# The layer norm's last step moved from VectorE to ScalarE in a transformer layer kernel

## The reference

```python
def _layernorm(x, axis=-1, eps=1e-05):
    m = jnp.mean(x, axis=axis, keepdims=True)
    v = jnp.var(x, axis=axis, keepdims=True)
    return (x - m) / jnp.sqrt(v + eps)
...
        q = _low_rank_proj(hidden_states, q_a, q_b)
        k = _low_rank_proj(hidden_states, k_a, k_b)
        v = hidden_states @ v_w.T + v_b
...
        att = jnp.where(causal[None, None], att, jnp.finfo(att.dtype).min)
        att = jax.nn.softmax(att, axis=-1)
        y = jnp.einsum('bhts,bhsd->bhtd', att, v)
...
    xn = _layernorm(x, axis=-1)
    x = x + _L0_attn_ref(xn, ...) + _L0_ffn_ref(xn, ...)
```

## Time and profile before

| | us |
|---|---|
| median of 3 runs (1224.98, 1230.92, 1231.64) | 1230.92 |
| the profiled execution, device time | 1225.27 |
| its span from first to last instruction | 1223.5 |
| PE busy | 1156.1 (94%) |
| DVE busy | 1012.4 (83%) |
| ACT busy | 683.7 (56%) |
| GpSimd busy | 699.0 (57%) |

### The profile page before, as it was taken

The page is one execution under the profiler, slowest core; times in us unless marked ns, Lnnn a source line. Parts: engine busy times, 40 slices in busy tenths (PEclk is TensorE's granted clock), DMA queues, the critical chain, the costliest instruction groups (busy, mean ns, idle before and its releaser), DMA issues. The chain is left out here.

```text
span 1223.5 us, 26313 instructions
## 1 busy us (share of the span) xinstructions
PE 1156.1 (94%) x8558; PEld 808.0 (66%) x8558; DVE 1012.4 (83%) x3396; ACT 683.7 (56%) x1334; POOL 699.0 (57%) x1021
## 2 busy tenths in 40 slices
PE   7799999999999999999999998889999999999994
PEld 6455565565555655555555554459889999999994
DVE  4798998989889999999999978779966777676762
ACT  4367667667667676767676665634333433343330
POOL 1235445445445344355355367755888888888874
PEclk9799999999999999999999999989999999999997
DMA  7534244244254343443442453225655665566753
GB/s 164 149 114 114 77 142 132 68 139 133 73 139 116 95 122 106 122 122 95 131 124 81 133 145 114 64 76 128 129 119 112 129 137 115 113 132 132 104 76 46
DMA packets 140380, 139.43 MB, mean 114 GB/s; under 512 B 24908, under 2 KB 132052, under 8 KB 140244
## 3 DMA queue, kind: packets, MB, share of 16 engines
q1 hardware_dynamic: 109540, 102.07, 29.3%
q0 software_dynamic: 24576, 33.57, 16.4%
q10 hardware_dynamic: 6128, 2.11, 0.8%
HBM read 53.22 MB, written 33.55 MB: 71 GB/s over the span
## 5 line engine op out<-in xcount | busy, mean ns | idle before, releaser
L850 DVE CUSTOM_DVE_ANT_0 junk<-bank,rowmask 128x256 bf16<-128x256 f32 (+3 forms) x1024 | 445.7, 481 | 33.4 <-PE bank L1016 30.1
L700 ACT ACTIVATE probs<-bank 128x512 f32<-128x512 f32 x640 | 365.4, 595 | 126.1 <-PE bank L1039 121.0
L585 POOL TENSOR_SCALAR_AFFINE_SELECT probs<-probs 128x256 f32<-128x256 f32 (+1 forms) x640 | 227.7, 370 | 237.4 <-ACT probs L700 232.9
L1016 PE MATMUL bank<-kstk,qstk 96*128 96x256 bf16 (+3 forms) x1024 | 247.7, 304 | 12.6 <-DMA kstk<-qk_part 6.9
L1039 PE MATMUL bank<-qstk,kstk 98*128 98x256 bf16 (+3 forms) x1024 | 249.1, 306 | 2.6 <-ACT probs L700 1.6
L1203 POOL DMA_INDIRECT out_rows<-mixed,rows x128 | 210.9, 1648 | 61.2 <-issue 36.6
L1061 PE MATMUL bank<-probs,vaug 128*32 128x512 f32 (+3 forms) x2048 | 180.5, 448 | 7.6 <-POOL probs L585 7.6
L1227 ACT ACTIVATE hid<-bank 128x512 f32<-128x512 f32 x128 | 76.6, 598 | 173.6 <-PE bank L1320 172.7
L1039 PEld LDWEIGHTS bank<-qstk,kstk 98*128 98x128 bf16 x1024 | 75.6, 98 | 137.3 <-ACT probs L700 92.7
L1338 PE MATMUL bank<-w_hi,hid_hi 128*128 128x256 f32 x512 | 147.3, 288 | 0.0
L1338 PE MATMUL bank<-w_hi,hid_lo 128*128 128x256 f32 x512 | 144.9, 283 | 0.0
(11 more groups left out here) (157 smaller groups left out, 2167.1 us busy)
## 6 DMA issues: line engine op xcount, KB each, us to landing
qstk<-qk_part SPq DMA_DIRECT2D x192, 128.0 KB, 2.4
kstk<-qk_part SPq DMA_DIRECT2D x186, 128.0 KB, 2.7
qstk<-in_L_ffn_w SPq DMA_DIRECT2D x32, 512.0 KB, 4.2
xln<-in_L_attn_hidden_states SPq DMA_DIRECT2D x16, 512.0 KB, 5.0
xn_rows<-xn SPq DMA_DIRECT2D x16, 512.0 KB, 2.9
xres<-in_L_attn_hidden_states SPq DMA_DIRECT2D x16, 512.0 KB, 4.0
out_rows<-xres SPq DMA_DIRECT2D x16, 512.0 KB, 3.4
out_rows<-mixed,rows POOLq DMA_INDIRECT x128, 3.9
```

The source lines that it names most:

```text
L585: nc.gpsimd.affine_select(out=block, in_=block, compare_op=ALU.is_ge, fill=0.0, base=0, pattern=[[0, len(cols)], [1, P]], channel_multipli ...
L700: nc.scalar.activation(probs[n % 2][:, 512 * k:512 * k + 512], SCORET[k % 2][:], ACT.Exp, scale=SCALE).then_inc(exp_done, 1)
L850: last = nc.vector.tensor_tensor_reduce(out=junk[k % 2][:, col:col + width], in0=SCORE[score_bank(UN * n + k)][:, col:col + width], in1=ro ...
L1016: last = nc.tensor.matmul(SCORE[score_bank(UN * n + k)][:, col:col + width], qstk[b % 2][0:KS, GH * g + h, P * i:P * i + P], kstk[b % 2][0 ...
```

## The change

DVE no longer writes `xn`. A new step `lnshift` on DVE forms shift = -mean * rstd in one small instruction of 128x4. `lnapply` is now ACT's: four activations with the function Identity, `xn = rstd * xln + shift`, where `rstd` and `shift` are one number per row. `lnshift` stands in slot 2 of g = 1, `lnapply` stays in slot 4. Who waits for `xn` (SP's store, PE's transposes) still waits for `xn_done`.

```diff
-    [(4, "lnapply", 2, 0), (6, "v", 1, 3), (6, "o", -1, 1), (7, "o", -1, 2), (8, "o", -1, 3)],
+    [(2, "lnshift", 2, 0), (4, "lnapply", 2, 0), (6, "v", 1, 3), (6, "o", -1, 1), (7, "o", -1, 2), (8, "o", -1, 3)],
...
-    ... + foldt(1) + [("lnapply", 0, 0), ("xload", 1, 0), ("warm", 8, 0)]
+    ... + foldt(1) + [("lnshift", 0, 0), ("lnapply", 0, 0), ("xload", 1, 0), ("warm", 8, 0)]
...
-    out += [("wo", 0, 0), ("wo", 1, 0), ("v", 0, 2), ("v", 0, 3), ("lnapply", 1, 0)]
+    out += [("wo", 0, 0), ("wo", 1, 0), ("v", 0, 2), ("v", 0, 3), ("lnshift", 1, 0), ("lnapply", 1, 0)]
...
@@ ScalarE @@
+                        elif kind == "lnapply":
+                            act.wait_ge(shift_done, n + 1)
+                            if n >= 1:
+                                act.wait_ge(xn_stored, 16 * n)
+                                prev = ("xt", n - 1, 1)
+                                act.wait_ge(shared_ready[bank_of(prev)], filled(prev, at))
+                            for tt in range(TT):
+                                last = nc.scalar.activation(xn[:, tt, :], xln[:, tt, :], ACT.Identity, bias=shift[:, tt:tt + 1],
+                                                            scale=rstd[:, tt:tt + 1])
+                            last.then_inc(xn_done, 1)
...
@@ VectorE @@
-                        elif kind == "lnapply":
-                            dve.wait_ge(rstd_done, at(n + 1, 2))
+                        elif kind == "lnshift":
+                            dve.wait_ge(rstd_done, n + 1)
                             if n >= 1:
-                                dve.wait_ge(xn_stored, at(16 * n, 32))
-                                prev = ("xt", n - 1, 1)
-                                dve.wait_ge(shared_ready[bank_of(prev)], filled(prev, at))
-                            for tt in range(TT):
-                                last = nc.vector.tensor_scalar(xn[:, tt, :], xln[:, tt, :], meanvar[:, tt, 0:1],
-                                                               rstd[:, tt:tt + 1], ALU.subtract, ALU.mult)
-                            last.then_inc(xn_done, 1)
+                                dve.wait_ge(xn_done, n)
+                            nc.vector.scalar_tensor_tensor(out=shift[:], in0=meanvar[:, :, 0], scalar=-1.0, in1=rstd[:],
+                                                           op0=ALU.mult, op1=ALU.mult).then_inc(shift_done, 1)
```

More of the change, by code:

```diff
@@ L130, in prologue_steps @@
     out = [("warm", 16, 0), ("xload", 0, 0)] + foldt(0) + [("lnstat", 0, 0), ("lnstat", 0, 1)]
-    out += [("foldm", 0, 0), ("fold", 0, 0), ("warm", 8, 0)] + foldt(1) + [("lnapply", 0, 0), ("xload", 1, 0), ("warm", 8, 0)]
+    out += [("foldm", 0, 0), ("fold", 0, 0), ("warm", 8, 0)] + foldt(1) + [("lnshift", 0, 0), ("lnapply", 0, 0), ("xload", 1, 0), ("warm", 8, 0)]
     out += foldt(2) + [("foldm", 1, 0), ("xt", 0, 0), ("xt", 0, 1), ("fold", 1, 0)] + foldt(3) + [("foldm", 2, 0), ("fold", 2, 0)]
@@ L325, in build @@
             vareps = sb("vareps", [P, TT], fp32)
-            rstd = sb("rstd", [P, TT], fp32)
+            rstd, shift = sb("rstd", [P, TT], fp32), sb("shift", [P, TT], fp32)
             ones_bf = sb("ones_bf", [P, H * T * SHIFT // P], bf16)
@@ L363, in build @@
             mv_done = sem("mv_done")
-            vareps_done = sem("vareps_done")
+            vareps_done, shift_done = sem("vareps_done"), sem("shift_done")
             rstd_done = sem("rstd_done")
```

## The result

The changed kernel took 1249.39 us (median of 4, 1245.55 to 1255.64) against 1231.28 us (median of 4) before: the medians are 18.1 us apart, and the ratio of the runs is 1.016 with a 95% interval of 1.0103 to 1.0218, slower. I had forecast 1241 us, slower, with a range of 1229 to 1253. Direction and mechanism held; the added time that I had summed, 12.6 us, is two thirds of what came. Two executions of the kernel before in a later job, at 1427 and 2226 us, fell in a slower state of the chip and are left out of every comparison.

The account below looks back on a forecast made before the run. PE was taken as nearly full (94% busy), with waits around lnapply deciding. Unranked 6.8, sequence 0 0.9, ranked 3.7 and prologue 1.2 make 12.6 us, added to the mean 1228.2: 1241 us, range 1229 to 1253.

Parts of the forecast that it names:

- The place and the path: Slots 4 to 7 of g = 1: ACT never idle, vaug late, PE loses 1.13 us at o part 2 per unranked sequence.
- D - 0.55 us: PE's loss at o part 2 per unranked sequence; D, the four activations' delay of ACT's next exponential, was put at 1.68 us.
- The price of one activation: ACT's new activation: 0.42 us from start to start, the nearest row without overlap; four make 1.68 us.
- The rival of dear operands: Each per-row operand lengthens ACT's activation: 0.48 us each, sum 16.5 us, time 1245 us; chance 0.25.
- The ranked sequences: Sequences 7 to 13: PE loses 1.13 us at o part 2, gets 0.6 back; 3.7 us in all.
- The give-back: Ranked sequences: of PE's 0.85 us of waits for DVE at L991 and L907, 0.6 us is returned per sequence.
- Sequence 0 and the prologue: Sequence 0: PE's slot 7 waits for the exponential of slot 5, 0.9 us; prologue: later xn, 1.2 us.
- The rival of a DVE-bound kernel: DVE sets the pace in ranked sequences, each 1.4 us shorter; with cheap operands 6 us faster, 1222; chance 0.12.
- the two levels of the times: The four times shown before lie at 1225 and 1231 us; the sum was added to their mean, 1228.2.

Follow-up runs that it names:

- e4: The changed kernel with the four activations behind v part 3 in slot 6 instead of in slot 4; 1235.28 us, ratio 1.0050.
- e8: The changed kernel with two entries of slot 6 exchanged, o part 1 before v part 3, so other parts share banks; 1238.53 us, ratio 1.0072.
- e2: The kernel before, DVE keeping lnapply, plus four spare ACT activations of the same size in slot 4 from sequence 2 on; 1247.17 us, ratio 1.0135.
- e3: The kernel before with one instead of four lnapply instructions on DVE from sequence 1 on, nothing added on ACT; 1225.57 us, ratio 0.9961.
- e5: The changed kernel with the four activations apart, in slots 4, 6, 7 and 8; 1230.26 us, ratio 1.0014.
- e7: The changed kernel with the shift per row only, the multiplication by rstd left out; 1242.92 us, ratio 1.0143.
- e9: The changed kernel, but sequences 0 to 2 keep DVE's lnapply; 1245.76 us, ratio 1.0113.

## Why the prediction was right, and what was too small

**The place and the path held.** ACT without slack in slots 4 to 7, `vaug` late, PE waiting at `o` part 2, 13 times, and in the unranked sequences nothing behind it that takes the delay in: the trace shows each. e4 takes away 1.33 and e8 0.96 of the 1.45 us by two edits that share only this wait. The formula D - 0.55 us gives 1.42 with the measured D, and `o` part 2 was 1.43 late.

**The price of one activation was mis-sized, and it is the term that made the sum too small.** I took 0.42 us from start to start; it is (2.06 - 0.59) / 3 = 0.49. The nearest rows hold no operand per row, and assuming only a lost overlap for them fell short. The rival of dear operands had 0.48 and 1245 us. The page "ScalarE: Activation LUTs" of the Trainium skill, section "What ACT_TABLE_LOAD costs", gives 93 ns per operand and an overlap of 93 ns, by which I had estimated 0.585 and 0.49 us; the traces agree (0.590, 92 ns per operand, 0.49). With D = 1.97 my own terms become 6 x 1.42 + 1.2 + 7 x 0.82 + 1.7 = 17.2 us, against 18.1 between the medians. The ratio's interval is wide, 13 to 27 us, so that the agreement to 1 us is in part luck; the agreement of the stretches is not.

**The ranked sequences kept more.** I let them keep 0.5 of the 1.1 us. They lose 1.54 us in g = 1 and 0.06 in g = 0, get 0.54 back later, and keep 1.06: 7.4 us where I had 3.7. The give-back itself, 0.54 for my 0.6, was right; it is the delay before it that was larger, 1.45 us in the stretch and not 1.13. The lighter DVE is not needed for it: e2, where DVE keeps all its work, gets 0.52 us back in the same two units (11.11 and 11.46 for 11.45 and 11.64). A PE that is late has less to wait for DVE.

**Sequence 0 and the prologue** were 0.9 and 1.2 us in my sum. Sequence 0 is 1.5 us longer (41.67 for 40.19). I had counted one wait there, and PE waits for ACT three times in a row, in slots 7, 8 and 9:

```profile
88.56 0.39 PE L1045 MATMUL bank<-qstk,kstk 98*128 98x256 bf16 x2 [1.04 <-ACT probs L710]
89.52 0.39 PE L1045 MATMUL bank<-qstk,kstk 98*128 98x512 bf16 x1 [0.35 <-ACT probs L710]
90.35 0.39 PE L1045 MATMUL bank<-qstk,kstk 98*128 98x384 bf16 x2 [0.22 <-ACT probs L710]
```

In the prologue the time from DVE's instruction to PE's first transpose of `xn` went from 1.61 to 2.41 us for sequence 0 and from 1.53 to 2.42 for sequence 1, 1.7 us together. How much of it reaches the end no profile shows: the first scores of the attention start anywhere from 56.4 to 63.1 us in the eleven profiles. With the local figures the terms are 6 x 1.45 + 7.4 + 1.5 + 1.7 = 19.3 us.

**The rival of a DVE-bound kernel** falls by e3's profile, 0.8 us in seven ranked sequences where it wanted 8, not by e3's time, whose interval reaches 9 us. **That only ACT's amount of work counts** was a rival of the experiments; e5 has all of it and is as fast as the kernel before, and its stretch is 5.82 us as there.

**What was not right** is my picture of the two levels of the times. I added to the mean of the four times shown, 1228.2; the median of before was 1230.2 to 1231.3 in all jobs. In one job its executions spread from 1219 to 1234 us, most of them from 1226 on, and show no two levels. So 3 us of the 8 that my 1241 was short come from the start and not from the sum.

## What to carry to other kernels

Before moving work to the engine with the lower busy share, look at the ten instructions around the place where it is to stand, and ask which of the results behind it another engine comes for without slack; here 13 us of spare time in each sequence were no help, since only 0.55 us of it lay between the new work and `vaug`'s reader. The same work cut in pieces and laid into the gaps that the listing shows cost PE nothing there, and the whole kernel was as fast as before. Compare a short stretch around the change before whole times: here it repeats to 0.08 us, where executions differ by more than 10. And price an operation by its operands too: two numbers per row made an activation of 256 elements half as dear again.

## What the runs showed of the hardware that I had not expected

ACT stands still right before the last `yraw`, for 7.0 to 7.2 us in seven of the ten profiles after the first, and for 3.8 us in the other three (e2, e4, e7); the profile before has no pause there. PE then waits 6.1 to 6.3 us in the seven, and is idle for 2.9 us at the same place in the three, against 0.8 before. From the first transposed scores of sequence 15 to the end it is 466.2 us before, 465.2 to 465.7 in the three, and 469.2 to 471.2 in the seven: with the short pause the end takes no longer than before, with the long one 3 to 5 us more. e3, whose ACT program is that of the kernel before, has the long one:

```profile
ACT yraw L704 <- remote: 7.0, 1, 7.0
PE bank L1070 <- ACT yraw L704: 10.9, 18, 6.1
```

The trace names no releaser, and what ACT waits for stays open. Whether this pause is behind the spread of the times of the kernel before stays open too, since no second profile of it was taken. The landing of `kstk` differs likewise, PE's wait for it being 6.9 to 12.3 us in all. In five places of the eleven profiles such a wait, 1.9 to 2.4 us long, was followed by 3.4 us of TensorE at half clock; other waits of 1.9 to 2.1 us (in e2, e8 and e9) were not. In sequence 3 it takes 8.8 us from the start of the unit to the exponential of slot 4 in the changed kernel, with a wait of 2.2 us and the half clock, and 7.2 us in e8, with a wait of 2.1 us and the full clock: the clock costs 1.6 us.
